# Attention products on TensorE mixed one by one, with scores and sums half a unit apart

## The reference, cut to what matters

```
qk     = einsum('nhcij,nhciw->nhijw', q, k) / D
qrq    = einsum('nhcij,chjw->nhijw', q, rq) / D
krk    = einsum('nhcij,chjw->nhijw', k, rk) / D
weight = softmax(qk + Gq * qrq + Gk * krk, axis=3)
out    = einsum('nhijw,nhciw->nhcij', weight, Gv1 * v) \
       + einsum('nhijw,chjw->nhcij', weight, Gv2 * rv)
```

## Time and profile before

| | us |
|---|---|
| median of 3 runs | 8297.43 (8284.11 to 8300.6) |
| profiled execution | 8291.75 |
| its span, first to last instruction | 8290.0 |
| PE busy in the span | 7187.2 (87%) |
| DVE busy | 5176.6 (62%) |
| ACT busy | 4856.3 (59%) |
| POOL busy | 2457.0 (30%) |
| mean granted TensorE clock | 0.749 of full |

### The profile page before, as it was taken

The page is one execution under the profiler, slowest core; times in us unless marked ns, Lnnn a source line. Parts: engine busy times, 40 slices in busy tenths (PEclk is TensorE's granted clock), DMA queues, the critical chain, the costliest instruction groups (busy, mean ns, idle before and its releaser), DMA issues. The chain is left out here.

```text
span 8290.0 us, 275612 instructions
## 1 busy us (share of the span) xinstructions
PE 7187.2 (87%) x106442; PEld 6044.4 (73%) x106442; DVE 5176.6 (62%) x20646; ACT 4856.3 (59%) x11427; POOL 2457.0 (30%) x1235
## 2 busy tenths in 40 slices
PE   4999999799999999999999899999999966766738
PEld 3555555689988888898899898898888932332338
DVE  5444444366666666666666666666666768988830
ACT  1444444577777777777777777777777733333410
POOL 0000000243443443444434444434434432322210
PEclk7999999666666666666666666666667688988855
DMA  7555555565655665655556656656656576766522
GB/s 217 203 203 204 204 204 197 113 112 100 112 103 98 113 107 101 107 99 107 101 106 112 102 100 109 109 99 110 105 100 109 92 232 203 265 201 202 208 74 99
DMA packets 1721071, 1148.11 MB, mean 138 GB/s; under 512 B 1143009, under 2 KB 1506145, under 8 KB 1703329
## 3 DMA queue, kind: packets, MB, share of 16 engines
q1 hardware_dynamic: 1530336, 842.56, 48.1%
q10 hardware_dynamic: 188352, 285.27, 9.3%
q0 software_dynamic: 1024, 2.09, 0.1%
HBM read 708.04 MB, written 421.56 MB: 136 GB/s over the span
## 5 line engine op out<-in xcount | busy, mean ns | idle before, releaser
L787 POOL TENSOR_TENSOR att_scores<-att_scores,att_inverse 128x1024 f32<-128x1024 f32 x1024 | 1966.8, 1934 | 2951.7 <-DVE att_inverse L722 2951.7
L660 ACT ACTIVATE att_scores<-att_scores,att_negmax 128x128 f32<-128x128 f32 x8192 | 2509.2, 399 | 67.6 <-issue 67.6
L737 DVE CUSTOM_DVE_ANT_0 att_scores<-att_ps,att_scores 128x128 f32<-128x128 f32 x8192 | 1780.8, 286 | 1066.7 <-PE att_ps L573 957.5
L560 PE MATMUL att_ps<-att_qk,att_rs 32*128 32x64 f32 x32768 | 1793.2, 380 | 155.6 <-ACT att_scores L652 114.2
L560 PEld LDWEIGHTS att_ps<-att_qk,att_rs 32*128 32x128 f32 x32768 | 1698.6, 299 | 196.2 <-ACT att_scores L652 142.5
L573 PE MATMUL att_ps<-att_own 16*128 16x128 f32 x16384 | 1541.6, 405 | 231.3 <-issue 224.1
L573 PEld LDWEIGHTS att_ps<-att_own 16*128 16x128 f32 x16384 | 1416.2, 300 | 268.9 <-issue 264.4
L652 ACT ACTIVATE att_scores<-att_ps 128x1024 f32<-128x1024 f32 x1024 | 992.4, 1021 | 1044.3 <-PE att_ps L560 1044.3
L720 DVE TENSOR_REDUCE att_total<-att_scores 128x8 f32<-128x1024 f32 x1024 | 1233.7, 1205 | 70.7 <-issue 70.7
L594 PE MATMUL att_ps<-att_scores,att_rv 128*16 128x64 f32 x32768 | 1249.6, 334 | 11.0 <-issue 10.8
L594 PEld LDWEIGHTS att_ps<-att_scores,att_rv 128*16 128x16 f32 x32768 | 1193.6, 127 | 24.5 <-issue 13.1
(11 more groups left out here) (146 smaller groups left out, 5276.0 us busy)
## 6 DMA issues: line engine op xcount, KB each, us to landing
qk<-proj_qk_out ACTq DMA_DIRECT2D x64, 2048.0 KB, 8.5
att_qk<-qk SPq DMA_DIRECT2D x512, 256.0 KB, 6.7
att_own<-qk SPq DMA_DIRECT2D x2048, 64.0 KB, 2.5
proj_x<-in_x_dram SPq DMA_DIRECT2D x128, 512.0 KB, 4.3
v_t<-proj_v_out ACTq DMA_DIRECT2D x64, 1024.0 KB, 11.3
att_vt<-v_t SPq DMA_DIRECT2D x128, 512.0 KB, 5.5
att_v<-att_att_v SPq DMA_DIRECT2D x512, 128.0 KB, 4.2
att_r<-att_att_r SPq DMA_DIRECT2D x512, 128.0 KB, 3.5
```

Source lines behind the costliest of these rows:

```text
L560: last = pe.matmul(ps[:, 4 + g, jj * IU:(jj + 1) * IU], rs[32 * g:32 * g + 32, t * JB + jj, :], qk[b][32 * g:32 * g + 32, :, t * JB + jj], ...
L660: last = act.activation(scores[v][:, i, :], scores[v][:, i, :], ACT.Exp, bias=negmax[v][:, i:i + 1], scale=-1.0)
L737: last = dve.tensor_tensor_reduce(out=scores[v][:, i, :], in0=ps[:, 2 * (p % 2) + r // 4, (r % 4) * W:(r % 4 + 1) * W], in1=scores[v][:, i ...
L787: pool.tensor_tensor(scores[v][:, rows, :], scores[v][:, rows, :], inverse[v][:, rows].unsqueeze(2).broadcast_to([P, PR, W]), ALU.mult).th ...
```

## The change

The products are the same in number and, but for the own scores, in shape. What changes:
- **Order on TensorE.** In place of two blocks per unit there are 64 short turns. A turn is one own score product, then 3, 2 or 0 relative ones, then 2 or 4 column products. A unit has four quarters q, and each has four kinds of turn, four of each kind: (1 own, 3 relative, 2 v), (1 own, 3 relative, 2 v, 2 rv), (1 own, 2 relative, 2 rv), (1 own, 4 rv).
- **Shift.** Quarters 0 to 2 of unit u carry relative rounds 1 to 3 of unit u+1, and quarter 3 carries round 0 of unit u+2. Quarters 0 and 1 carry sums 2 and 3 of unit u-2, quarters 2 and 3 carry sums 0 and 1 of unit u-1.
- **Own scores** use 32 array rows: the tiles `own` are zeroed once at the start, and the loads fill the first 16 of each 32 partitions as before, so the added rows are zeros. A piece has 4 rows on one row group (PR = 4, 16 pieces), in bank 0 or 1. Relative scores take banks 2 to 5, v sums bank 6, rv sums bank 7.
- **ACT and DVE** take pieces of 4 rows with an exponential two pieces behind; sums and inverses still go by 8 rows. DVE copies all v sums, ACT all rv sums.
- **SP** loads `vt` in two halves and `rv` in four parts, and stores `att_v` and `att_r` in halves, 16 stores per unit in place of 8. `att_r` is laid out in pieces of 16 columns (JT = 16) in place of 32, and the combining stage reads it so.

```diff
-PR = 8
+PR = 4
+SR = 8
+SPIECES = IU // SR
-JT = JG
+JT = JG // 2
+STORES_G = JG // JT
...
-            def own_scores(u, p):
-                half, block16 = p // (PIECES // 2), (p % (PIECES // 2)) // 2
...
-                for r in range(4):
-                    for gg in range(2):
-                        g = 2 * (p % 2) + gg
-                        at = block16 * 4 + r
-                        last = pe.matmul(ps[:, g, r * W:(r + 1) * W], own[half][32 * g:32 * g + HD, 1, at, :], own[half][32 * g:32 * g + HD, 0, at, :],
-                                         start=True, stop=True, tile_position=(32 * g, 0))
...
+            def own_score(u, p, r):
+                half, g = p // (PIECES // 2), p % G
...
+                at = (p // G) % (HROWS // 16) * PR + r
+                last = pe.matmul(ps[:, p % 2, r * W:(r + 1) * W], own[half][32 * g:32 * g + 32, 1, at, :], own[half][32 * g:32 * g + 32, 0, at, :],
+                                 start=True, stop=True, tile_position=(32 * g, 0))
...
+            def unit(u, v, parts):
+                back2, back1, now, ahead1, ahead2 = parts
+                for q in range(4):
+                    rel_on, sums_on = (ahead1, ahead1, ahead1, ahead2)[q], (back2, back2, back1, back1)[q]
+                    ru, rt = (u + 1, q + 1) if q < 3 else (u + 2, 0)
+                    rb = v + 1 if q < 3 else v + 2
+                    su, sb, b = (u - 2, v - 2, q + 2) if q < 2 else (u - 1, v - 1, q - 2)
+                    for x in range(PR):
+                        if now:
+                            own_score(u, 4 * q, x)
+                        if rel_on:
+                            relative(ru, rb, rt, range(3 * x, 3 * x + 3))
+                        if sums_on:
+                            sums_with_v(su, sb, b, range(2 * x, 2 * x + 2))
+                    for x in range(PR):
+                        if now:
+                            own_score(u, 4 * q + 1, x)
+                        if rel_on:
+                            relative(ru, rb, rt, range(12 + 3 * x, 15 + 3 * x))
+                        if sums_on:
+                            sums_with_v(su, sb, b, range(8 + 2 * x, 10 + 2 * x))
+                            sums_with_r(su, sb, b, range(2 * x, 2 * x + 2))
+                    for x in range(PR):
+                        if now:
+                            own_score(u, 4 * q + 2, x)
+                        if rel_on:
+                            relative(ru, rb, rt, range(24 + 2 * x, 26 + 2 * x))
+                        if sums_on:
+                            sums_with_r(su, sb, b, range(8 + 2 * x, 10 + 2 * x))
+                    for x in range(PR):
+                        if now:
+                            own_score(u, 4 * q + 3, x)
+                        if sums_on:
+                            sums_with_r(su, sb, b, range(16 + 4 * x, 20 + 4 * x))
...
+            for half in range(2):
+                dve.memset(own[half][:, :, :, :], 0.0).then_inc(cleared, 1)
+            dve.memset(ps[:, 6:8, :], 0.0).then_inc(cleared, 1)
```

More of the change, by code:

```diff
@@ L529, in _ @@
                 load_qk(0, k)
+            sp.wait_ge(cleared, 2)
             for half in range(2):
@@ new lines, in relative @@
+            def relative(u, v, t, steps):
+                if 0 in steps:
+                    if t == 0:
+                        pe.wait_ge(qk_loaded[v % 2], 64 * (u // 2) + 64)
+                    if t % (ROUNDS // 2) == 0:
+                        pe.wait_ge(rs_ready[t // (ROUNDS // 2)], u // UPH + 1)
+                    later(pe, rel_read, ROUNDS * u + t)
+                for x in steps:
+                    jj, g = x // G, x % G
+                    last = pe.matmul(ps[:, 2 + g, jj * IU:(jj + 1) * IU], rs[32 * g:32 * g + 32, t * JB + jj, :],
+                                     qk[v % 2][32 * g:32 * g + 32, :, t * JB + jj], start=True, stop=True, tile_position=(32 * g, 0))
+                if JB * G - 1 in steps:
+                    last.then_inc(rel_done, 1)
@@ new lines, in sums_with_v @@
+            def sums_with_v(u, v, b, steps):
+                if 0 in steps:
+                    if b % (FILLS // 2) == 0:
+                        pe.wait_ge(v_loaded[b // (FILLS // 2)], 16 * u + 16)
+                    if b == 0:
+                        pe.wait_ge(normed, SPIECES * u + SPIECES)
+                    later(pe, v_read, FILLS * u + b)
+                for x in steps:
+                    r, g = x // G, x % G
+                    i = 16 * b + 4 * r + g
+                    last = pe.matmul(ps[32 * g:32 * g + HD, 6, r * W:(r + 1) * W], vt[i // HROWS][:, i % HROWS, :], scores[v % BUFS][:, i, :],
+                                     start=True, stop=True, tile_position=(0, 32 * g))
+                if 15 in steps:
+                    last.then_inc(v_done, 1)
@@ new lines, in sums_with_r @@
+            def sums_with_r(u, v, b, steps):
+                if 0 in steps:
+                    pe.wait_ge(rv_loaded[b], (u // UPH) * 16 + 16)
+                    later(pe, r_read, FILLS * u + b)
+                for x in steps:
+                    jj, g = x // G, x % G
+                    j = g * JG + b * JB + jj
+                    last = pe.matmul(ps[32 * g:32 * g + HD, 7, jj * IU:(jj + 1) * IU], rv[:, j, :], scores[v % BUFS][:, :, j],
+                                     start=True, stop=True, tile_position=(0, 32 * g))
+                if JB * G - 1 in steps:
+                    last.then_inc(r_done, 1)
```

341 lines of the change are left out of this document (130 added, 211 removed).

## The result

The changed kernel takes 14,647.74 us (median of 4 runs, 14,641.48 to 14,649.42), the kernel before 8,293.69 beside it (8,284.11 to 8,300.6): ratio 1.766 [1.763, 1.769]. The forecast was 15,390 with a range of 10,300 to 16,600, so the direction and the range held, and the size was 742 us (5%) too high.

A forecast was written before the change was run, and what follows sets the result against it. TensorE was taken as the bound. Replacing the attention's 5058 us by 12,020 and adding 100 + 20 + 20 to the profiled 8292 gave 15,394, so 15,390 us, range 10,300 to 16,600.

The forecast's parts named there:

- The drain: Row-column changes on TensorE: the next kind waits until the last product is nearly out, 0.23 to 0.35 us at 1.2 GHz.
- The lower bound: Change into row products: at least 0.20 us with the weight load hidden, 2,950 us less in all.
- The half clock throughout: TensorE in the attention: 1.2 GHz in all turns, 93.9 us per unit, 12,020 us in all.
- the change behind rv: Wait after an rv product before row products begin: 0.26 us, from 0.335 - 0.07.
- the start of the row part: Own score instructions opening each turn: two loads of 0.21 us on one group before the second's product.
- the added terms: Outside the turns: 100 us for PE's waits on issue, 20 for the last unit's sums, 20 for the combining stage.
- The stalls at jumps: PE's waits on issue, once a loop round: 100 of 224 us kept as added time.
- The ends: End of the attention: the last unit's sums finish half a unit later, 20 us added.
- The one at the full clock: Rival for the attention: changes cost as forecast but at 2.4 GHz, 58.7 us a unit, total 10,880 us; chance 0.14.
- the likeliest case: Changes wait for the array to empty, at 1.2 GHz: 15,390 us, own range 13,000 to 16,700; chance 0.72.
- Free changes: Rival: frequent row-column changes cost nothing, without overlap, at 2.4 GHz: total about 8,480 us; chance 0.04.
- overlap between row and column products: Rival: both kinds run together in the array at 2.4 GHz, ACT bounds, total about 7,470 us; chance 0.10.

The follow-up runs named there:

- dense_block: The changed kernel with ten dense 128 x 128 products added at the start of each unit, turns unchanged: 15,242.3 us, 1.837 of the kernel before.
- turn_per_piece: The changed kernel with 16 turns per unit in place of 64, each a whole piece: 8779.6 us, 1.060 of the kernel before.
- two_turns_a_piece: The changed kernel with 32 turns per unit in place of 64, each piece split in two: 11,885.6 us, 1.433 of the kernel before.
- before_own32: The kernel before with only its own scores widened to 32 array rows, the added ones zeros: 8234.9 us, 0.994 of the kernel before.
- quarter_mixed_rows: `turn_per_quarter` with own and relative products alternating within the row part, two pieces finished together: 8680.6 us, 1.046 of the kernel before.
- quarter_balanced: `turn_per_quarter` with a 16-unit loop, earlier gains and table scaling, and two relative products of other row groups after each own score: 7466.8 us, ratio 0.900.
- turn_per_quarter: The changed kernel with 4 turns per unit, all own and relative products of a quarter, then its sums: 8258.9 us, 0.998 of the kernel before.

## Why the prediction was right, and where its sizes were off

**The drain** (most of the working rests on it). The next kind starts the last product's duration less 0.07 us after that product. Measured after, at a clock of 0.50: v to own 0.351 (0.35 used), relative to v or rv 0.331 from the start of a product of 0.401 (0.23 used), own to v and rv 0.346 (0.34), rv to own 0.230 (0.26). At a clock of 1.00 it is 0.20 after v and own (`dense_block`), 0.21 after relative ones, and after rv 0.22 in `dense_block` and 0.26 in `turn_per_piece`. That the array empties at a change is a reading of these starts; the traces give the size of the gap, as far as starts and modelled ends can. The lower bound, a load hidden at the change, is refuted by PEld's 8095 waits, 0.27 us each.

**The clock.** The half clock throughout was right (0.50 over the 11,407 us). The two parts of the loss can now be told apart: the same 64 turns at a clock of 1.00 take 58.7 us per unit (`dense_block`), at 0.50 88.9. Of the 49.4 us over the old mean unit of 39.5, 30.2 are the clock's, and 19.2 would be left at the full clock. The old unit ran at a mean clock of 0.68, so the 19.2 understate the order's own cost: at the full clock, 64 turns take 24.6 us more than 4 turns (34.1), for the drains and the groups left empty together, which no run parts. The cause of the half clock was argued from the density of the stretch; `dense_block` shows that the mix loses a full clock, and `turn_per_piece` against `two_turns_a_piece` that the same products in longer runs have it most of the time (0.89 against 0.51). The prediction's step from a mix that is nowhere "as dense as the block that raised the clock" to the half clock gave the right clock here, but mixing as such does not decide: 16 turns a unit are a mix too, with 32 changes. An instruction in flight is not enough for the full clock: PE was busy 11,272 of the 11,407 us, at 0.50.

**The sizes.** By kind, measured against predicted: 1.51 and 1.55, 1.72 and 1.82, 1.215 and 1.33, 1.116 and 1.17, together 5.56 and 5.87, which is 88.9 and 93.9 us per unit. Times 128 this is 640 of the 742 us. The mis-sized terms are the second rv instruction behind the first on a group (0.10 to 0.12, where 0.15 was taken from the long block of the earlier trace rows), the change behind rv, and the start of the row part: the second own instruction starts 0.375 behind the first, where load and step were put at 0.42. That makes 0.72 for 0.76 where no group is shared. With a shared group it is 1.04 for 1.07, but by luck: the last relative product starts 0.71 behind the first own one, where four loads of 0.21 made 0.84, and its change costs 0.33 where 0.23 was used. Half the columns did not make it shorter by 0.11: a relative instruction lasts 0.401, an own one 0.416, and the prediction's own rule, with the 0.40 that it read in the earlier trace rows, gives 0.33. The remaining 100 us are the added terms, and there two errors partly cancel. The stalls at jumps cost more than the 100 us put down: each of the two units beside a jump is about 2.7 us longer, some 155 us in all. The ends cost less: the attention, from first to last sum, is some 125 us shorter than 128 full units and these stalls, since its last turns hold sums alone, where 20 us were added. And what follows the attention did not grow, where 20 us were added. One reading was wrong without weight: slice 23 of the earlier trace rows is at 8 tenths, not over 90%.

**The rivals.** The one at the full clock was priced at 58.7 us a unit, and that is what the turns take when the clock is there; it fell on the clock alone. The stated range took in both clocks, so holding the range says little; the likeliest case's own range, 13,000 to 16,700, held too, though its lower end did not follow the working, which gives 15,394 - 2,950 = 12,444. Free changes and overlap between row and column products fell on the gaps: in no timeline read here does a row product start before the last column product is within 0.07 us of its end.

**What stays open.** No run settles which property of a stretch decides its clock. The number of turns, the active rows (`before_own32`) and the order within the row part (`quarter_mixed_rows`) all move it; only the rows were varied at a constant order, and by little. Short stops in each quarter do not decide it by themselves (`quarter_balanced`). That the 16 zero rows act by filling the array is argued; only the clock and the time were seen.

## What to carry to other kernels

Mix products that use the array in the same way (here own and relative scores, both on row groups), choosing the next one from another group, and let the pieces finish one after the other: `quarter_mixed_rows`, which finished two together, lost 422 us to `turn_per_quarter`, for a reason that is open. Change between row and column groups a few times per unit at most, since in these runs the product behind a change started no more than 0.07 us before the modelled end of the one ahead of it, and an own score behind it also had its weight load in the open (PEld idle for 0.27 us before it, 8095 times in the changed kernel). Then price a stall of the array with the clock behind it (in `turn_per_quarter` 13.7 to 20.5 us at 0.50 go with each wait over 2 us), and take loop jumps and once-a-head waits out first: a loop of 16 units and earlier gains alone gave 313 us here. The overlap is real within a kind: it gave 414 us, and the fastest kernel, at 7434 us, is 10.3% under the kernel before.

## What the runs showed of the hardware that was not expected

- Sixteen rows of zeros in the own scores made the kernel before 0.6% faster, at a granted clock of 0.71 for 0.68 in the attention, and made no difference where the clock was 0.50 anyway (14,642.5 us without them, 14,647.74 with them).
- A mix of row and column products held a granted clock of 0.89 with 16 turns a unit, and 0.51 with 32, with the same products.
- At a change the next product starts 0.07 us before the last one's modelled end (0.069 to 0.071 at all changes of the kernel after between 2000 and 12,900 us), at a clock of 0.50 and, in `dense_block`, of 1.00, and after all four kinds of product.
- Stops of PE of 0.4 to 0.5 us, once in nearly every quarter, went with a mean clock of 0.74 in `quarter_mixed_rows` and of 0.93 in `quarter_balanced`: stops as short as these did not by themselves bring the clock down.
